# Keys of a token block turned in 32x32 blocks on VectorE and placed by transfers; convolution taps multiplied on ScalarE into PSUM and added on VectorE

## What is computed

```python
xn = layernorm(x)
q, k, v = split(xn @ wqkv); q, k = relu(q), relu(k)          # 16 heads of 16
kv  = cumsum(k[..., :, None] * v[..., None, :], axis=2)      # causal linear attention
num = einsum('bhnd,bhnde->bhne', q, kv)
den = einsum('bhnd,bhnd->bhn', q, cumsum(k, axis=2))[..., None] + EPS
attn = (num / den) @ wo
# mixture of experts on xn: 8 scores, top 2, 4 MLP experts, 3 that pass x or relu(x) on, 1 that adds nothing
routed = sum_e cw[:, e] * (silu(xn @ Wg[e]) * (xn @ Wu[e])) @ Wd[e] + (cw4 + cw6) * xn + cw7 * relu(xn)
shared = depthwise_causal_conv(xn, conv_w, 4 taps) + conv_b
out = x + attn + routed + shared
```

## Time and profile before

| | |
|---|---|
| median of 3 runs | 1308.19 us (1307.94 to 1309.42) |
| the profiled execution | 1308.92 us, span 1307.1 us |
| TensorE (PE) busy | 1287.2 us, 98% |
| VectorE (DVE) busy | 1144.3 us, 88% |
| GpSimd (POOL) busy | 830.8 us, 64% |
| ScalarE (ACT) busy | 707.8 us, 54% |
| TensorE clock granted, mean | 0.999 |

### The profile page before, as it was taken

One profiled execution on the slowest core, in us unless ns is written; L12 is line 12 of the kernel. 1 busy time (PEld: TensorE's weight loads), 2 busy tenths in 40 slices (PEclk: granted clock), 3 DMA queues, 4 the chain that ended last, 5 costly groups with the idle time before them and its releaser, 6 DMA issues.

```text
span 1307.1 us, 55818 instructions
## 1 busy us (share of the span) xinstructions
PE 1287.2 (98%) x24160; PEld 1116.5 (85%) x24160; DVE 1144.3 (88%) x2686; ACT 707.8 (54%) x1487; POOL 830.8 (64%) x673
## 2 busy tenths in 40 slices
PE   5999999999999999999999999999999999999998
PEld 4888888888888888888888888888888888888887
DVE  7988898888898888988888988889888889888885
ACT  5645655455654456554555544565545555445552
POOL 2676665765666756657656667566576566675554
PEclk9999999999999999999999999999999999999999
DMA  5012212222222222222222222221222222222211
GB/s 185 14 56 73 78 50 51 80 78 78 65 61 56 79 78 79 51 51 81 78 79 64 67 51 78 78 78 51 51 80 78 79 64 67 51 78 63 61 35 34
DMA packets 175860, 88.54 MB, mean 68 GB/s; under 512 B 135552, under 2 KB 171264, under 8 KB 171520
## 3 DMA queue, kind: packets, MB, share of 16 engines
q1 hardware_dynamic: 174912, 83.97, 22.6%
q10 hardware_dynamic: 704, 1.01, 0.2%
HBM read 53.18 MB, written 17.04 MB: 54 GB/s over the span
## 4 chain that ended last, share of the span: by engine, by line
PE 95%; DVE 3%; POOL 1%; issue 1%; ACT 0%; DMA 0%; DVEq 0%; POOLq 0%
PE ring L343 51%; PE scores L343 17%; PE ring L466 7%; PE ring L482 6%; PE scores L415 5%; PE state_sum L429 4%; PE ring L488 2%; PE scores L397 2%; DVE sm L895 1%; POOL xn L731 0%; DMA x_t<-in_L_attn_x_dram 0%; PE scores L352 0%; POOL rstd L722 0%; DVE stats L819 0%; POOL x_t L748 0%
## 5 line engine op out<-in xcount | busy, mean ns | idle before, releaser
L757 POOL TENSOR_TENSOR hid<-hid,cwb 128x512 f32<-128x512 f32 x128 | 166.4, 1300 | 181.8 <-DVE hid L924 181.0
L916 DVE SCALAR_TENSOR_TENSOR cT<-xT,conv_ws,cT 128x512 f32<-128x512 f32 x192 | 275.1, 1471 | 0.0
L745 POOL TENSOR_TENSOR x_t<-x_t,same 128x1024 f32<-128x1024 f32 x32 | 76.9, 2404 | 254.9 <-ACT same L618 254.9
L639 ACT ACTIVATE sg<-ring 128x512 f32<-128x512 f32 x128 | 76.6, 599 | 268.5 <-PE ring L343 268.5
L343 PE MATMUL ring<-xl,wgu_h 128*128 128x512 f32 x512 | 213.1, 416 | 0.0
L761 POOL TENSOR_TENSOR hl<-hid,hh 128x512 fp32r<-128x512 f32 x128 | 208.8, 1632 | 0.0
L343 PE MATMUL ring<-xh,wgu_l 128*128 128x512 f32 x512 | 201.0, 393 | 0.3 <-issue 0.3
L343 PE MATMUL ring<-xh,wgu_h 128*128 128x512 f32 x512 | 200.5, 392 | 0.0
L569 ACT ACTIVATE yh<-yT 128x256 fp32r<-128x256 f32 x128 | 53.5, 418 | 246.7 <-DVE yT L933 246.7
L902 DVE TENSOR_TENSOR state_bd<-state_sum,tables_s 128x256 f32<-128x256 f32 x248 | 104.0, 419 | 93.8 <-PE state_sum L429 90.6
L895 DVE TENSOR_TENSOR sm<-scores,causal_s 128x512 f32<-128x512 f32 x256 | 157.7, 675 | 6.0 <-PE scores L415 5.0
(11 more groups left out here) (134 smaller groups left out, 3453.4 us busy)
## 6 DMA issues: line engine op xcount, KB each, us to landing
cwb<-cw_rows SPq DMA_DIRECT2D x32, 1024.0 KB, 4.6
x_t<-in_L_attn_x_dram SPq DMA_DIRECT2D x32, 512.0 KB, 4.2
out_dram<-x_t SPq DMA_DIRECT2D x31, 512.0 KB, 2.9
xT<-qks_tok SPq DMA_DIRECT2D x896, 16.0 KB, 1.8
cw_rows<-cwt SPq DMA_DIRECT2D x128, 2.0 KB, 1.4
sm<-in_L_attn_wqkv_dram ACTq DMA_DIRECT2D x2, 384.0 KB, 5.0
sm<-in_L_ffn_Wg_dram SPq DMA_DIRECT2D x2, 256.0 KB, 3.8
sm<-in_L_ffn_Wu_dram SPq DMA_DIRECT2D x2, 256.0 KB, 4.6
```

What stands on the lines that cost most here:

```text
L639: act.activation(sg[:, :], GB[t % 2], ACT.Silu).then_inc(s_sg, 1)
L745: pool.tensor_tensor(xb, xb, same[:, :, :], ALU.add).then_inc(s_base1, 1)
L757: pool.tensor_tensor(hid[:, e, :], hid[:, e, :], cwb[:, e, :], ALU.mult).then_inc(s_hid, 1)
L916: ins = dve.scalar_tensor_tensor(out=cT[:, c, :], in0=xT[:, third(s, j, 0), c, LEAD - HALO + n:LEAD - HALO + n + BT], scalar=conv_ws[:, c, ...
```

## The change

1. **Keys.** For `k = 1`, TensorE turns only tiles 0 and 1 (4 transposes in place of 8), and ScalarE copies only these. Tiles 2 and 3 are turned by VectorE in 32x32 blocks (`turn_keys`: two transposes of 128x256, behind the router) into the free row `hid[:, 2]`, and SyncE places the blocks in `ktok` by 16 transfers of 16 KB (`place_keys`: 4 before `cwb` is read back, 12 after it). TensorE waits for them ahead of `state_sum(4)`, VectorE before it writes `hid[:, 2]` again.
2. **Convolution.** In 28 batches (the fourth to the last but one) ScalarE multiplies each of taps 1 to 3 (`tap_terms`, two instructions of 128x512) into the PSUM banks `TB = SB[0:2]`, and VectorE adds them to `cT` (`add_terms`, two tensor-tensor additions in place of two of L916). TensorE waits for the last addition ahead of the key projections of `heads`.
3. **Transfers.** Of the 32 of `place_turned`, SyncE keeps 24; 8 are issued on ScalarE's queue, 4 behind `tap_terms(1)` and 4 behind `tap_terms(2)`.
4. **FILL** goes from 38 to 52, and the waits stand in two halves of 26: at the head of the batch and ahead of `gate_up(2)`.

```diff
-    FILL = 38
+    FILL = 52
...
+        kb = hid[:, 2, :].rearrange("p (a t g i) -> p a t g i", a=QUADS, t=2, g=C)
...
+        TB = SB[0:2]
...
                     sp.dma_start(cw_rows[:, bs], cwt[b * BLK:b * BLK + E * T, :]).then_inc(cw_out, 16)
+                if k:
+                    place_keys(s, j, k, range(1))
                 sp.wait_ge(cw_out, at(s, j, 16 * P // BLK, (k + 1) * 16 * P // BLK))
...
+            def place_keys(s, j, k, quarters):
+
+                sp.wait_ge(s_kturn, at(s, j, 1, k))
+                for a in quarters:
+                    for q in range(QUADS):
+                        sp.dma_start(ktok[a * BLK:(a + 1) * BLK, 2:4, :, q * BLK:(q + 1) * BLK],
+                                     kb[q * BLK:(q + 1) * BLK, a, :, :, :]).then_inc(ktok_in, 16)
...
                 if left > 1 and by_blocks(s, j, 2):
-                    place_turned(s, j, 2)
+                    place_turned(s, j, 2, 0, range(QUADS))
+                    place_turned(s, j, 2, 1, range(QUADS // 2))
                 if left:
                     spread_cw(s, j, 1)
+                    place_keys(s, j, 1, range(1, QUADS))
                     sp.wait_ge(s_out, at(s, j, T, 2 * T))
...
+                if k and by_blocks(s, j, k):
+
+                    pe.wait_ge(s_conv, at(s, j, HALO, HALO))
                 for g in range(C):
                     project(KB[g][:, :], D + g * P).then_inc(s_kp, 1)
...
-                    for t in range(T):
+
+                    for t in range(T // 2 if k else T):
                         ins = nc.tensor.transpose(KTB[g][:, t * P:(t + 1) * P], kT[:, g, t * P:(t + 1) * P],
...
                 t, h = n // 2, n % 2
+                if n == T and s + j:
+
+                    pe.wait_ge(ktok_in, keys_at(s, j, k))
...
-                if not last and by_blocks(s, j, 1):
-
-
-                    for _ in range(FILL):
-                        pe.wait_ge(tables_in, 16)
-                for t in range(T):
+                def fill(n):
+
+
+                    if not last and by_blocks(s, j, 1):
+                        for _ in range(n):
+                            pe.wait_ge(tables_in, 16)
+
+                for t in range(T):
+                    if t % 2 == 0:
+                        fill(FILL // 2)
                     gate_up(t)
...
+            def place_turned(s, j, a):
+
+                act.wait_ge(s_turn, at(s, j, 1, 3 - BY_PE))
+                act.wait_ge(s_halo, at(s, j, 1, 1))
+                for q in range(QUADS):
+                    row = xT[q * BLK:(q + 1) * BLK, third(s, j, 2), 1, LEAD:LEAD + BT]
+                    act.dma_start(row.rearrange("p (t a n) -> p t a n", t=T, a=QUADS)[:, :, a, :],
+                                  xb_t[a * BLK:(a + 1) * BLK, 1, q, :, :]).then_inc(xT_in[1], 16)
...
+                def tap_terms(n):
+
+                    if n == 1:
+
+                        act.wait_ge(s_sm, at(s, j, U * ROWS, U * ROWS))
+                    else:
+                        act.wait_ge(s_conv, at(s, j, HALO, n - 1))
+                    for c in range(C):
+                        first = LEAD - HALO + n
+                        ins = act.activation(TB[c][:, :], xT[:, third(s, j, 0), c, first:first + BT], ACT.Copy,
+                                             scale=conv_ws[:, c, n:n + 1])
+                    ins.then_inc(s_tapped, 1)
...
                 high_hid(0)
+                if ahead:
+                    tap_terms(1)
+                if left > 1 and by_blocks(s, j, 2):
+                    place_turned(s, j, 2)
                 high_y(1)
...
                 high_hid(1)
+                if ahead:
+                    tap_terms(2)
+                if left > 1 and by_blocks(s, j, 2):
+                    place_turned(s, j, 3)
                 high_y(2)
                 silu(3)
                 high_hid(2)
+                if ahead:
+                    tap_terms(3)
                 high_y(3)
...
+            def turn_keys(s, j, k):
+
+                for g in range(C):
+                    dve.wait_ge(s_kT, at(s, j, C, k * C + g + 1))
+                dve.wait_ge(s_hl, at(s, j, T, 3))
+                for t in range(2):
+                    ins = dve.transpose(kb[:, :, t, :, :].rearrange("p a g i -> p g a i"),
+                                        kT[:, :, (2 + t) * P:(3 + t) * P].rearrange("p g (a n) -> p g a n", n=BLK))
+                ins.then_inc(s_kturn, 1)
...
+                def add_terms(n):
+
+                    if n == 1:
+                        dve.wait_ge(s_tap0, at(s, j, 1, 1))
+                    else:
+                        dve.wait_ge(s_conv, at(s, j, HALO, n - 1))
+                    dve.wait_ge(s_tapped, (s * BPS + j - BY_PE + 1) * HALO + n)
+                    for c in range(C):
+                        ins = dve.tensor_tensor(cT[:, c, :], TB[c][:, :], cT[:, c, :], ALU.add)
+                    ins.then_inc(s_conv, 1)
+
                 def tap(n):
+                    if not last and by_blocks(s, j, 1):
+                        add_terms(n)
+                        return
...
+                    if t == 2 and s + j:
+
+                        dve.wait_ge(ktok_in, keys_at(s, j, 0))
                     dve.tensor_tensor(hid[:, t, :], UB[t % 2], sg[:, :], ALU.mult).then_inc(s_gu, 1)
...
                     router(s, j, 1)
+                    turn_keys(s, j, 1)
                     key_sums(s, j, 1)
```

More of the change, by code:

```diff
@@ L202, in layer_kernel @@
         s_ktok = sem("s_ktok")
+        s_kturn = sem("s_kturn")
+        ktok_in = sem("ktok_in")
         s_qp = sem("s_qp")
@@ L225, in layer_kernel @@
         s_conv = sem("s_conv")
+        s_tapped = sem("s_tapped")
         s_op = sem("s_op")
@@ L250, in by_blocks, with keys_at @@
             return s * BPS + j + k >= BY_PE
+        def keys_at(s, j, k):
+            return (s * BPS + j + k) * (16 * QUADS * QUADS)
         def third(s, j, k):
@@ L300, in spread_cw, with place_turned @@
                              cw_rows.rearrange("r n -> (r n)").partition_broadcast(P)).then_inc(cw_in, 16)
-            def place_turned(s, j, k):
+            def place_turned(s, j, k, c, quarters):
                 sp.wait_ge(s_turn, at(s, j, 1, k + 1 - BY_PE))
                 sp.wait_ge(s_halo, at(s, j, 1, k - 1))
-                for c in range(C):
-                    for a in range(QUADS):
-                        for q in range(QUADS):
-                            row = xT[q * BLK:(q + 1) * BLK, third(s, j, k), c, LEAD:LEAD + BT]
-                            sp.dma_start(row.rearrange("p (t a n) -> p t a n", t=T, a=QUADS)[:, :, a, :],
-                                         xb_t[a * BLK:(a + 1) * BLK, c, q, :, :]).then_inc(xT_in[c], 16)
+                for a in quarters:
+                    for q in range(QUADS):
+                        row = xT[q * BLK:(q + 1) * BLK, third(s, j, k), c, LEAD:LEAD + BT]
+                        sp.dma_start(row.rearrange("p (t a n) -> p t a n", t=T, a=QUADS)[:, :, a, :],
+                                     xb_t[a * BLK:(a + 1) * BLK, c, q, :, :]).then_inc(xT_in[c], 16)
+            def place_keys(s, j, k, quarters):
+                sp.wait_ge(s_kturn, at(s, j, 1, k))
+                for a in quarters:
+                    for q in range(QUADS):
+                        sp.dma_start(ktok[a * BLK:(a + 1) * BLK, 2:4, :, q * BLK:(q + 1) * BLK],
+                                     kb[q * BLK:(q + 1) * BLK, a, :, :, :]).then_inc(ktok_in, 16)
             def batch(s, j, left):
@@ L612, in heads @@
                     act.wait_ge(s_ktr, at(s, j, C, k * C + g + 1))
-                    copy(ktok[:, :, g, :], KTB[g][:, :].rearrange("p (t n) -> p t n", t=T)).then_inc(s_ktok, 1)
+                    some = T // 2 if k else T
+                    copy(ktok[:, 0:some, g, :], KTB[g][:, 0:some * P].rearrange("p (t n) -> p t n", t=some)
+                         ).then_inc(s_ktok, 1)
+            def place_turned(s, j, a):
+                act.wait_ge(s_turn, at(s, j, 1, 3 - BY_PE))
+                act.wait_ge(s_halo, at(s, j, 1, 1))
+                for q in range(QUADS):
+                    row = xT[q * BLK:(q + 1) * BLK, third(s, j, 2), 1, LEAD:LEAD + BT]
+                    act.dma_start(row.rearrange("p (t a n) -> p t a n", t=T, a=QUADS)[:, :, a, :],
+                                  xb_t[a * BLK:(a + 1) * BLK, 1, q, :, :]).then_inc(xT_in[1], 16)
             def same_terms(s, j, k):
```

## The result

| | median | span of the profiled execution |
|---|---|---|
| before | 1308.49 us (1307.94 to 1309.42, 4 runs) | 1307.1 |
| after | 1325.24 us (1325.00 to 1325.52, 4 runs) | 1323.6, at a granted clock of 0.998 |

The changed kernel is slower: ratio 1.0127, 95% interval 1.0110 to 1.0145, which is +16.75 us where the sum said +9.7. The page shows the same kind of kernel as the earlier trace rows: TensorE from end to end.

A forecast was written before the change was run, and what follows sets the result against it. The prediction took TensorE's queue as the bound. Its terms, -13.5 (transposes) + 21.6 (second FILL half) + 1.6 (wait for the keys) = +9.7 us, put 1308.19 at 1318 us, range 1295 to 1337.

The forecast's parts named there:

- the right side: Whole kernel: the changed kernel was forecast to be slower, with a chance of 0.67.
- The path: Whole batch: it costs what TensorE's queue costs, 40.00 us; relieving VectorE is worth nothing by itself.
- Transposes, -13.5: Key transposes on TensorE: four fewer, 0.109 us each, in 31 batches save 13.5 us.
- FILL, first half, 0: Head of the batch: 13 wait instructions are covered by queued matmuls of 256 columns and cost 0.
- FILL, second half, +21.6: Ahead of gate_up(2), behind 16 short matmuls: 13 wait instructions stop TensorE for 0.77 us in 28 batches, +21.6 us.
- The wait for the keys, +1.6: Ahead of state_sum(4): one extra wait instruction on TensorE, 0.05 us in 31 batches, +1.6 us.
- Keys landing, VectorE: Keys land before state_sum(4) with 2.0 us in hand, cost 0; VectorE's added transposes before the key sums cost 0.
- ScalarE, 0 to 0.2 and 0 taken: ScalarE's taps and four transfers, 3.0 us, ahead of silu(2): 0 to 0.2 us a batch, hidden by TensorE's stall.
- The hidden second half: Rival ahead of gate_up(2): the second FILL half costs nothing, so the kernel gets faster, 1296 us; chance 0.26.
- the late keys: Rival at state_sum(4): TensorE waits for keys that land late, 1346 us if 1 us late; chance 0.04.
- The rival with ScalarE's silu late: Rival at silu(2): ScalarE's transfers hold it up, sg comes 1.7 us late in 28 batches, 1366 us; chance 0.06.
- That rival's sum of 6.1 us: ScalarE's four transfers ahead of silu(2), each waiting for one of SyncE's: 8 x 0.76 = 6.1 us.

The follow-up runs named there:

- g: The kernel before with only the convolution taps on ScalarE and the additions on VectorE: 1308.23 us, ratio 0.9996.
- f: The kernel before without its 38 FILL waits (FILL = 0): 1318.71 us, ratio 1.0077.
- e: The changed kernel without any of its 52 FILL waits (FILL = 0): 1326.02 us, ratio 1.0128 against the kernel before.
- d: The kernel before with its 38 FILL waits split, 12 at the batch head and 26 ahead of gate_up(2): 1330.41 us, ratio 1.0163.
- c: The changed kernel with the second half of FILL ahead of output(1) and ScalarE's eight transfers in four pairs: 1303.22 us, ratio 0.9957 against the kernel before.
- h: Kernel a with all 32 transfers of the turned inputs issued by SyncE: 1359.57 us, ratio 1.0370 against the kernel before.
- k: Kernel a with six of ScalarE's transfers behind its last copy of the fourth tile, two behind the first key activation: 1431.04 us, ratio 1.0921.
- i: Kernel h with the last four transfers on ScalarE behind its second tap, 28 on SyncE: 1303.31 us, ratio 0.9963 against the kernel before.
- j: Kernel a with both of ScalarE's groups, eight transfers, behind its second tap: 1337.34 us, ratio 1.0216 against the kernel before.
- a: The changed kernel with the second half of FILL moved from ahead of gate_up(2) to ahead of output(1): 1309.52 us, ratio 1.0003 against the kernel before.
- l: The kernel before with eight of SyncE's 32 transfers issued by ScalarE at the places the change gives them: 1320.25 us, ratio 1.0083.
- b: The changed kernel with ScalarE's eight transfers in four pairs, behind its three taps and first key activation: 1325.85 us, ratio 1.0129 against the kernel before.

## Why the prediction was right, and where its sum was off

The forecast had the right side and the right main cost; that the time fell within its range is in part luck. The range was wide for the second half of FILL, and a good part of what it had to cover came from ScalarE's transfers, which had been put at nothing.

**The path.** Right: TensorE's queue alone sets the time, and VectorE's relief is worth nothing (g, ratio 0.9996).

**Transposes, -13.5.** Right: 0.44 us a batch less, -0.45 in the stage, -14.2 over the two traces.

**FILL, first half, 0.** Right by its cost: tile 0 takes 5.69 us with 26 waits and 5.71 with 38. What the prediction didn't see is what they do: without them tile 0 costs 0.35 to 0.70 us more (f, e).

**FILL, second half, +21.6.** The mechanism was right and d shows it by itself. The term was too small: 0.83 (d) to 0.88 us a batch (the second matmul 1.83 us behind L512 against 0.95), which is 23.2 to 24.6 us, and tile 1 has +24.2 over the whole trace. In the changed kernel the first of the waits is executed 0.02 to 0.17 us behind the start of L512 (at 570.03 in the batch shown, 0.14 behind), with 11 to 14 of its 16 matmuls still to start, where the prediction put it at the start and had some 16; in d it is 0.02 behind, with 14 to start, in all of batches 4 to 29.

**The wait for the keys, +1.6.** Not there: c, h and k have this wait and not the waits of FILL beside it, and their tile 1 takes 4.72, 4.71 and 4.70 us against 4.72 before. The 0.01 to 0.03 more in i, j and a is at most 0.8 us of the whole. **Keys landing, VectorE**: right, no wait for either is in the lists.

**ScalarE, 0 to 0.2 and 0 taken.** This step failed. Its words were that the stalled TensorE itself hides ScalarE's delay, and the delay is indeed mostly hidden (one open wait for sg, 0.4 us). But the transfers cost in a way that the prediction didn't have: issued along with SyncE's, just ahead of and beside tile 2's small matmuls, these come further apart, 0.24 us at tile 2, +6.4 us. l shows it without the rest of the change (203.8 to 217.6 us in the two groups), h and k (203.0 and 204.2) its absence where ScalarE issues none there. The step was also sized too small: the four transfers held ScalarE's queue for 4.2 us and not 3.0.

With the terms as the two traces have them: -14.2 + 24.2 + 6.4 + 0.1 = +16.5 us of span, +16.75 in the medians. Of the 7 us missing in the forecast, 6.4 are ScalarE's transfers and 2.6 the second half of FILL, less 1.6 for the key wait and 0.7 for the transposes.

**The rivals.** The hidden second half is refuted by d, and the late keys did not come. The rival with ScalarE's silu late was wrong at its place in the change, and its kind of loss came in j (34.5 us of waits for `sg`) and, at the values in place of silu, in k, where more transfers stand in front of needed work. That rival's sum of 6.1 us had each of the four issues wait for one of SyncE's; the four took 4.2. In k six of ScalarE's issues took 4.18 us, from 579.69 on, while SyncE issued five of its own (580.06 to 583.53, 0.59 to 0.60 each): side by side, and not in turns at 0.76 us each. The three that took 3.60 us in the changed kernel hold one long issue, 2.03 us at 569.64, beside a long one of SyncE's, 1.87 at 569.79; but SyncE has long ones of 1.48 and 1.34 us without ScalarE too (k, at 568.43 and 573.18).

**Still open.** Why the small matmuls come further apart when two queues issue (1.34 us in place of 1.08 at tile 2), and why they don't with a fetch just ahead of the numerators (1.08 to 1.09 in l). The loss outlasts the issues; that it comes from what the transfers do behind them is my guess, which no run tested. Why tile 2 takes 5.14 us in a and 4.95 in the changed kernel is in part the open waits for `sg` (2.4 us in all); the rest was not tested. Nor was a version found in which ScalarE's eight transfers lie beside large matmuls without delaying the values.

## What to carry to other kernels

Count what a change does to the number and the place of the instructions of the bounding engine, waits that are long satisfied among them: here 26 and 38 of them cost nothing behind matmuls of 256 columns (tile 0 at 5.69 and 5.71 us), and 26 behind sixteen matmuls of 64 columns cost 0.83 us (d). Before waits that compute nothing are moved or dropped, take the same count modulo 256 and see what lies where a break was seen, for the waits may be padding: without them f had 8 breaks among its small matmuls (6.7 us), and lost 10 us. A second queue for transfers was not free either, even with its engine in time (11 us in l). Beside large matmuls its issues left the small ones alone (204.2 us in k), but there they held up what ScalarE owed next (88 us of waits), so look at both when you place them.

## What the runs showed of the hardware that was not expected

- 38 satisfied waits, themselves hidden, save 10 us (f), by keeping one place in each 256 of TensorE's instructions (all 19 breaks in e and f lie at 193 or 194) away from 64 matmuls of 128 columns.
- Eight transfers of 16 KB issued by ScalarE in place of SyncE cost 11 us in an otherwise unchanged kernel (l). The small matmuls come further apart behind ScalarE's issues too, when these are nearly over (b, c: 1.18 us against 1.08 at tile 2, 1.03 against 0.88 at tile 3).
- Behind a stretch in which TensorE was busy for 1.12 of 3 us, its granted clock was 0.67, 0.50, 0.50 and 0.62 in the four windows of 1 us from 600 on (k). With the stall of 0.84 us in each batch of the changed kernel nothing of the kind shows: its clock was 0.998 over the span.
